# Two convolution layers on one core: another placing of rows on partitions in the first layer, and loads, stores and masks moved in the second

## The reference, cut to what matters

```python
def reference(x, L0_conv_weight, L0_conv_bias, L1_conv_conv_w, L1_conv_conv_b):   # x (8, 32, 512, 512) f32
    x = x + layer0(groupnorm16(x))     # 3x3 conv on rounded int8 values, bias, rounded and clipped to int8
    x = x + layer1(groupnorm16(x))
# layer0: x_q = clip(round(v / 0.05)), w_q = clip(round(w / 0.01)); conv 3x3, padding 1;
#         out = clip(round((acc * 0.0005 + bias) / 0.1)) * 0.1
# layer1: feat = 1x1 conv of v (32 -> 32) + bias; filt = feat pooled to 5x5 for each image and channel
#         (adaptive bins; neighbouring bins share a row where 512/5 is no integer);
#         out = depthwise 5x5 conv of feat, padding 2, each image and channel with its own filt
```

## Time and profile before

| | |
|---|---|
| median of 3 runs | 6000.67 us (5993.56 to 6012.33) |
| the profiled execution | 5992.25 us |
| its span | 5990.5 us |
| busy: PE, DVE, ACT, POOL | 4829.2, 4582.7, 3994.4, 1384.6 us |
| moved by DMA | 1347.06 MB |
| first layer; between; second | 0 to 2581 us; to 2642; to 5990 |

### The profile page before, as it was taken

How to read it: one execution, slowest core, us unless ns; L and a number is a source line. 1 busy time by engine, 2 the same in 40 slices (tenths; PEclk the granted TensorE clock), 3 DMA queues, 4 the chain that set the end, 5 groups by cost and what they waited for, 6 DMA issues and landing times.

```text
span 5990.5 us, 113135 instructions
## 1 busy us (share of the span) xinstructions
PE 4829.2 (81%) x43798; PEld 3263.0 (54%) x43798; DVE 4582.7 (76%) x5363; ACT 3994.4 (67%) x2509; POOL 1384.6 (23%) x1698
## 2 busy tenths in 40 slices
PE   0767767666667767918998989989989899899899
PEld 0111111111111111207988979979979789799798
DVE  6787878777787878747887868868868778688686
ACT  1646565655555556807877868868868778688686
POOL 0111111111111111112332323323323333233233
PEclk9888878888888888958999999989999999999999
DMA  9999999999999998949999999999999999999997
GB/s 263 278 276 301 301 287 302 281 302 273 319 261 322 271 312 242 287 96 184 180 196 179 180 193 183 181 190 182 188 192 180 197 179 180 188 189 178 188 190 125
DMA packets 1065164, 1347.06 MB, mean 225 GB/s; under 512 B 78330, under 2 KB 636666, under 8 KB 1060602
## 3 DMA queue, kind: packets, MB, share of 16 engines
q1 hardware_dynamic: 749506, 657.45, 49.3%
q0 software_dynamic: 240000, 537.11, 39.9%
q10 hardware_dynamic: 75072, 144.72, 8.3%
HBM read 800.10 MB, written 538.84 MB: 224 GB/s over the span
## 4 chain that ended last, share of the span: by engine, by line
PE 48%; SPq 4%; DMA 2%; DVE 0%; issue 0%; POOL 0%; ACT 0%; DVEq 0%; POOLq 0%; ACTq 0%
PE c_tps L1074 36%; PE c_cps L1053 4%; PE c_cps L1054 4%; PE c_cps L1055 4%; SPq L851 3%; DMA c_tt<-bias_scratch 2%; SPq L871 1%; DMA c_x<-out_dram 1%; DVE c_z L998 0%; POOL c_feat L907 0%; ACT c_z L966 0%; DVE c_xr L1031 0%; POOL c_starter L904 0%; POOL out_dram L925 0%; ACT c_feat L979 0%
## 5 line engine op out<-in xcount | busy, mean ns | idle before, releaser
L1074 PE MATMUL c_tps<-c_feat,c_tt 123*128 123x256 f16 (+1 forms) x20736 | 2385.6, 273 | 169.3 <-DMA c_tt<-bias_scratch 167.5
L1074 PEld LDWEIGHTS c_tps<-c_feat,c_tt 123*128 123x128 f16 (+1 forms) x20736 | 1998.8, 98 | 428.1 <-DMA c_tt<-bias_scratch 134.8
L925 POOL DMA_DIRECT2D out_dram<-c_xr x1152 | 1056.5, 1054 | 2266.3 <-DVE c_xr L1031 2105.9
L440 PE MATMUL b_ps<-b_xq,w0main 128*128 128x512 bf16 x3072 | 950.1, 415 | 679.5 <-ACT b_q L398 540.3
L966 ACT ACTIVATE c_z<-c_x,c_rs 128x976 f16<-128x976 f32 x576 | 1150.2, 1997 | 116.1 <-DMA c_x<-out_dram 116.1
L1031 DVE TENSOR_SCALAR c_xr<-c_tps 57x1024 f32<-57x1024 f32 (+1 forms) x576 | 701.5, 1218 | 686.1 <-PE c_tps L1074 686.1
L998 DVE SCALAR_TENSOR_TENSOR c_z<-c_x,c_rs,c_z 128x976 f16<-128x976 f32 x576 | 1105.9, 1920 | 69.6 <-ACT c_z L966 47.0
L398 ACT ACTIVATE b_q<-b_ps,q_bias 128x1024 int8<-128x1024 f32 x512 | 547.6, 1115 | 787.3 <-DVE b_x L518 728.8
L988 ACT ACTIVATE c_xr<-c_tps 57x1024 f32<-57x1024 f32 (+1 forms) x576 | 639.2, 1110 | 629.0 <-PE c_tps L1074 628.9
L440 PEld LDWEIGHTS b_ps<-b_xq,w0main 128*128 128x128 bf16 x3072 | 225.6, 101 | 1351.3 <-issue 1094.1
L453 PE MATMUL b_ps<-b_xq,w0edge 64*32 64x512 bf16 x3048 | 918.5, 411 | 0.0
(11 more groups left out here) (131 smaller groups left out, 2732.2 us busy)
## 6 DMA issues: line engine op xcount, KB each, us to landing
out_dram<-b_x POOLq DMA_DIRECT2D x512, 512.0 KB, 11.2
out_dram<-c_xr POOLq DMA_DIRECT2D x576, 384.0 KB, 7.9
c_x<-out_dram SPq DMA_DIRECT2D x224, 976.0 KB, 21.9
b_stream<-in_x_dram SPq DMA_DIRECT2D x672, 256.0 KB, 12.7
b_x<-in_x_dram ACTq DMA_DIRECT2D x276, 512.0 KB, 13.3
b_x<-in_x_dram SPq DMA_DIRECT2D x276, 512.0 KB, 12.4
c_tt<-table_scratch SPq DMA_DIRECT2D x64, 576.0 KB
out_dram<-c_xr POOLq DMA_DIRECT2D x512, 72.0 KB, 9.2
```

The costliest lines, as they stand in the source:

```text
L440: return pe.matmul(ps[:, g % 3, j, :], k.w0main[:, d, :, :].rearrange("p r o -> p (r o)"), xq[:, n % XQ_SLOTS, 2 * i + j, d:d + W], start= ...
L925: pool.dma_start(out[e::2][p, 4 * s:4 * s + 4, r0 + lo:r0 + hi, :].rearrange("c h w -> h c w"), xr_rows(m, lo, hi), accum_op=ALU.add).then ...
L1074: last = pe.matmul(tps[:, s % 2, o % 4, :], tt[0:rows, o, tp, 2 * d:2 * d + 2, :].rearrange("k w m -> k (w m)"), feat[0:rows, (e * N + i) ...
```

## The change

- **First layer.** Partition 4c+r now holds channel c's rows of image quarter r (128 rows each), so that a chunk is 8 neighbouring rows of each of the four quarters. A contiguous run is 16 KB for a whole chunk and 8 KB for half of one. A chunk is loaded by two transfers of 128 partitions (1 MB each; SP the first four rows, ACT the others), the stream by one for each half, and stored by one of 2 MB.
- All taps of a row now lie in the same partition group: 9 full 128x128 matmuls a row. At the quarters' seams the row above or below comes from a halo, `xh`: twice an image three 2 KB-a-partition transfers of 32 partitions from SP, and two ACT instructions of one row.
- Masks, group matrices and the sums' bookkeeping follow the new placing. The segments of rows, and so the number of DVE instructions in the first layer, stay as they are (edges at 25, 51, 76 and 102 of 128 both before and after). In `filters` the five bins are now gathered by quarter: 40 dependent instructions in place of 13. The weights are loaded in four transfers behind the others, after a memset.
- **Between the layers.** The first two x blocks' loads, the fillings of `feat` and `z` and the start of the store semaphores move into `statistics_of_x1`.
- **Second layer.** `z` has 3 slots, ACT works 3 steps ahead, DVE 2. SP's order where the image changes: groups 0 and 1, x block, groups 2 and 3. A step's 57 rows are stored by one transfer.

```diff
-Z_SLOTS = 4
+Z_SLOTS = 3
...
-        xv = x.rearrange("b c (n j r) w -> b n r c j w", j=JB, r=4)
+        xv = x.rearrange("b c (r n j) w -> b n (c r) j w", j=JB, r=Q)
...
-        def load_chunk(eng, xv, b, n, rows):
-            s = n % X_SLOTS
-            for r in rows:
-                eng.dma_start(xt[C * r:C * r + C, s, :, :], xv[b, n, r, :, :, :]).then_inc(x_loaded[s], 16)
+        def load_chunk(eng, xv, b, n, h):
+            s, rows = n % X_SLOTS, slice(JB // 2 * h, JB // 2 * (h + 1))
+            eng.dma_start(xt[:, s, rows, :], xv[b, n, :, rows, :]).then_inc(x_loaded[s], 16)
+
+        def load_halo(eng, xv, b, h):
+            for r in range(1, Q):
+                eng.dma_start(xh[r - h::Q, :], xv[b, :, QH * r - 1 + h, :]).then_inc(halo_loaded, 16)
...
-                            for r in range(Q):
-                                sp.dma_start(xs[C * r:C * r + C, h, :, :],
-                                             next_x[b, RESIDENT + n, r, :, JB // 2 * h:JB // 2 * (h + 1), :]).then_inc(stream_loaded[h], 16)
+                            sp.dma_start(xs[:, h, :, :],
+                                         next_x[b, RESIDENT + n, :, JB // 2 * h:JB // 2 * (h + 1), :]).then_inc(stream_loaded[h], 16)
...
-                            inner(0, True, False)
-                            for d in range(3):
-                                    pe.matmul(ps[0:C, g % 3, j, :], k.w0edge[P // 2:P, d, :],
-                                    pe.matmul(ps[P - C:P, g % 3, j, :], k.w0edge[0:P // 2, d, :],
-                            inner(1, False, False)
-                            last = inner(2, False, True)
+                            for y in (1, 0, 2):
+                                for d in range(3):
+                                    last = pe.matmul(ps[:, g % 3, j, :], k.w0main[:, y, d, :, :].rearrange("p o r -> p (o r)"),
+                                                     row(2 * i + j + y - 1)[:, d:d + W], start=(y == 1 and d == 0), stop=(y == 2 and d == 2))
...
-                    for r in range(Q):
-                        pool.dma_start(x1v[b, n, r, :, :, :], xt[C * r:C * r + C, s, :, :]).then_inc(x1_stored[s], 16)
+                    pool.dma_start(x1v[b, n, :, :, :], xt[:, s, :, :]).then_inc(x1_stored[s], 16)
...
+            for j in range(2):
+                load_block(sp, buffers, j, x1v[0], j)
...
             for i in range(NBINS):
+                for r in range(Q):
+                    for m in range(NSEG):
+                        if i not in bins_of(r, m):
+                            continue
+                        quarter = k.quarter[:, r:r + 1]
...
-                    if pointwise and j == N and s in (5, 7):
-                        sp.wait_ge(band_done, count(p, e, TILES, TILES - STEPS + s - 3) + START)
-                        load_table(p, e + 1, (s - 5) // 2)
+                    if pointwise and j == N and s in (2, 4):
+                        sp.wait_ge(band_done, count(p, e, TILES, TILES - STEPS + s) + START)
+                        load_table(p, e + 1, s // 2 - 1)
+                    if s == 6 and pointwise and (j + 2 < N or another(p, e)):
+                        load_x1(sp, p, e, j + 2)
...
-                    for lo, hi in ((0, SPLIT), (SPLIT, n)):
-                        pool.dma_start(out[e::2][p, 4 * s:4 * s + 4, r0 + lo:r0 + hi, :].rearrange("c h w -> h c w"),
-                                       xr_rows(m, lo, hi), accum_op=ALU.add).then_inc(stored[m % XR_SLOTS], 16)
+                    pool.dma_start(out[e::2][p, 4 * s:4 * s + 4, r0:r0 + n, :].rearrange("c h w -> h c w"),
+                                   xr_rows(m, 0, n), accum_op=ALU.add).then_inc(stored[m % XR_SLOTS], 16)
```

More of the change, by code:

```diff
@@ L84, with bins_of, bins_of_row @@
 NG = len(GROUPS)
+def bins_of(r, seg):
+    t = J_SEGS[seg][0]
+    assert all(bins_of_row(QH * r + t) == bins_of_row(QH * r + u) for u in range(*J_SEGS[seg]))
+    return bins_of_row(QH * r + t)
+def bins_of_row(row):
+    return [i for i in range(NBINS) if edges(i)[0] <= row < edges(i)[1]]
 SEG_GROUPS = [[g for g, t in enumerate(GROUPS) if t[3] == n] for n in range(NSEG)]
@@ L116, in _ @@
+            for r in range(Q):
+                sp.dma_start(w0f[r::Q, r, :, :], w0.rearrange("o c h w -> c o (h w)")).then_inc(spread, 16)
         @block.gpsimd
         def _(pool):
[L120 to L135, removed]
@@ new lines, in blocks @@
+            def blocks(mask, view, rows, pattern, value):
+                pool.memset(mask[:, :], value).then_inc(pool_chain, 1)
+                steps[0] += 1
+                for sign, base in ((1, 0), (-1, rows - 1)):
+                    pool.wait_ge(pool_chain, steps[0])
+                    m = view(mask[:, :])
+                    pool.affine_select(out=m, in_=m, compare_op=ALU.is_ge, fill=0.0, base=base,
+                                       pattern=[[sign * a, b] for a, b in pattern],
+                                       channel_multiplier=sign).then_inc(pool_chain, 1)
+                    steps[0] += 1
@@ L150, in link @@
                 dve.wait_ge(chain, steps[0])
-            dve.memset(k.w0main[:, :, :, :], 0.0)
-            dve.memset(k.w0edge[:, :, :], 0.0)
+            dve.memset(w0f[:, :, :, :], 0.0).then_inc(zeroed, 1)
             dve.memset(k.wh[:, :, :], 0.0)
             link(dve.memset(k.wf[:, :, :], 0.0))
-            for i in range(NBINS - 1):
-                for r in range(Q):
[L159 to L162, removed]
             for a in range(NBINS):
@@ L606, in _ @@
             gs.vector_means(dve, 0, own)
+            for slot in range(2):
+                dve.memset(feat[96:P, slot, 1, :, :], 0.0).then_inc(filled, 1)
             gs.vector_spread(dve, 0, own)
@@ L610, in _ @@
             dve.tensor_copy(rstd[:, :], gs.rstd[:, :])
-            dve.tensor_copy(mean[:, :], gs.mean[:, :]).then_inc(kept, 1)
+            dve.tensor_copy(mean[:, :], ps[:, 2, 0:nb]).then_inc(kept, 1)
+            for t in range(Z_SLOTS):
+                dve.memset(z[:, t, :, :, MAIN:P].rearrange("p b c d -> p (b c) d"), 0.0)
             dve.wait_ge(kept, 1 + START)
@@ L754, in _, with __init__, sb, rows_in @@
             sp.wait_ge(stored, 16 * (5 * lots + 1))
-def depthwise(nc, nb, k, rstd, table_d, bias_d, out):
+class BlockBuffers:
+    def __init__(self, nc, ctx):
+        def sb(name, shape, dt):
+            return ctx.enter_context(nc.sbuf_tensor(name, shape, dt))
+        self.xt = sb("c_x", [P, 2, ROWS_IN, P], F32)
+        self.z = sb("c_z", [P, Z_SLOTS, 2, PAIRS_PART, P], F16)
+        self.feat = sb("c_feat", [P, 2, 2, C, FP], F16)
+        self.starter = sb("c_starter", [P, XR_SLOTS], F32)
+        self.x1_loaded = [ctx.enter_context(nc.semaphore(f"c_x1_loaded{i}")) for i in range(2)]
+        self.stored = [ctx.enter_context(nc.semaphore(f"c_stored{i}")) for i in range(XR_SLOTS)]
+def rows_in(i):
+    return (2 if i == 0 else 0), min(ROWS_IN, H + 2 - ROWS_OUT * i)
+def load_block(eng, buffers, slot, x1, i):
+    lo, hi = rows_in(i)
+    r0 = ROWS_OUT * i - 2
+    for q in range(Q):
+        eng.dma_start(buffers.xt[C * q:C * q + C, slot, lo:hi, :], x1[q, :, r0 + lo:r0 + hi, :]).then_inc(buffers.x1_loaded[slot], 16)
+def depthwise(nc, nb, k, rstd, buffers, table_d, bias_d, out):
     with ExitStack() as ctx:
```

301 lines of the change are left out of this document (173 added, 128 removed).

## The result

The changed kernel takes 5950.0 us (median of 6 runs, 5939.1 to 5970.4) against 6001.6 (6 runs): a ratio of 0.9917, 95% interval 0.9898 to 0.9936. It is 0.8% faster, where 5.9% was forecast and 5560 us was the near end of the range, 5850 the far one. The span of the profiled execution falls by 45.7 us, from 5990.5 to 5944.8.

What follows compares the result with a forecast made beforehand. Transfers were taken to bound the streaming images, PE the last. From 5992.25 us, -20 - 279 + 56 + 2 - 38 - 74 = -353 gave 5639, and 8.4 for the runs' median gave 5647 us, range 5560 to 5850.

Steps and rivals of the forecast that it cites:

- One store of 57 partitions: Second layer: storing a step's rows in one transfer costs nothing while it ends within 21 us.
- rival 3: Second layer: the 57-partition store runs on few DMA engines, 18 to 28 us, costing beyond about 20; chance 0.10 for slower.
- PE's pitch and floor: First layer: full matmuls 0.215 us apart, so every image takes at least 247.7 + 21.4 = 269 us.
- the last image: First layer's final image, which streams nothing: grows from 213 to 269 us, a loss of 56 us.
- Transfers in the first layer: Streaming images: longer runs put transfers below PE's floor, 277 us an image for 316.8, -279 us over seven.
- The line through packet sizes: First-layer DMA: 27 ns plus 0.041 ns a byte per packet, giving 295 GB/s at 2 KB, 361 at 8 KB.
- First pass and start: First layer's beginning: first pass 100 us for 120, -20; start +2 for weights and a wider rounding.
- Between the layers: Statistics and filters: +13 fillings, +9 filters, -41 earlier first split; with block 2's x -19, sum -38 us.
- the 27 instructions: Added dependent instructions in `filters`, 0.29 us each with gaps of 0.04: +9 us.
- The second wait, for block 2's x: Second layer's beginning: ACT's 19.3 us wait for that block's load taken as gone, -19 us.
- Change of image: Second layer: SP's new order moves PE's table wait from step 2 to step 4, 7 x 10.6 = -74 us.
- the lookahead: Second layer: `z` with 3 slots and ACT and DVE working further ahead, priced at zero.

Runs made afterwards that it cites:

- kernel 8: Changed kernel with stores as 48 and 9, first-layer transfers over 128 partitions but every second row (stores every fourth), runs of 2 KB: 5632.5 us.
- kernels 7 to 9: Changed kernel, stores as 48 and 9; first-layer transfers as four of 32 neighbouring partitions, 2 KB runs over 128, four of every fourth partition: 6072.3, 5632.5, 5623.0 us.
- kernel 1: Changed kernel with only the one-piece store undone, a step's 57 rows again stored as 48 and 9: 5636.3 us.
- kernel 11: Changed kernel with stores as 48 and 9, first x blocks' loads and the fillings moved from the statistics into the filters' block: 5625.5 us.

## Why the prediction was wrong, point by point

- **The step that failed** is "One store of 57 partitions moves the same bytes; while a step's store ends within the cycle of 4 `xr` slots, 4 x 5.3 = 21 us, it costs nothing". A store costs its largest engine's share of the rows, not its bytes. 57 has no divisor between 3 and 19, so 3 of 16 DMA engines carry it; alone it takes 16.5 us, in the kernel 19.5 to landing. The condition was wrong as well: 19.5 is below the cycle of 21, and it still cost 314 us in the changed kernel and 324 in the kernel before. In the changed kernel's trace a slot's cycle has, besides the store, 1.2 us of writing, 0.8 to POOL's issue and 0.7 from landing to the next writing (medians). That leaves 18.5 of 21.2 us for the store, and a quarter of the stores take over 20.8. It was rival 3 with its mechanism, but not with its price: by its 20 us a store of 19.5 would have been free too. I gave it 0.10, although the pair 48 and 9 in the code and the factors of 57 were both before me and no row spoke against it. At 19.5 us it left a gain of 0.8%, a case for which the range had no room.
- **PE's pitch and floor**: right. 0.216 us, image 264.6 to 269 forecast; the last image pays 51 of 56.
- **Transfers in the first layer**: the size is right (273 for 277, the floor 269 set a little high), the reason wrong. The line through packet sizes gave 361 GB/s for 8 KB and 295 for 2 KB; kernel 8 moves 2 KB runs at 387, and as fast as the image needs. What decided was how a transfer's partitions are spread (kernels 7 to 9), which I had left outside the sum. That transfers fell below PE's floor all the same, and the size with it, is luck.
- **First pass and start**: -17.5 for -18.
- **Between the layers**: -8 for -19. I let SP's eight loads of x go free. SP needs 33 us to issue them, and the block didn't end before:

```profile
2311.43 33.36 SPq L869 DMA_DIRECT2D c_x<-out_dram  x8
...
2327.82 0.90 DVE L688 COPY mean<-s_ps 128x8 f32<-128x8 f32 x1
...
2345.26 0.09 DVE L746 MEMSET f_blank<- 1x32 uint32 x1 [16.54 <-PEq L642]
```

The statistics are done at 2328.7, `filters` begins at 2345.3. The rest is 6 us better than forecast in all, the 27 instructions (9 us) as forecast. The second wait, for block 2's x, fell from 19.3 us to 3.3 in kernel 1.
- **Change of image**: 74 us were credited to the order. The order as changed is worth nothing; the lookahead, which I priced at zero, is worth 38. The x block's turn in SP's queue comes when DVE has read the last of the old one, and that comes a step earlier. With the stores in two, the second layer gained 78 us in all for the 93 forecast: 38 from the lookahead, 16 from block 2's x, and the rest in shorter waits for tables (167 to 144 us with order and lookahead undone), whose cause stays open.

With the store undone the same sum would have met 5636 with 5647. That is luck: 74 us too many for the order stand against 38 too few for the lookahead, 25 too few for the streaming images and the open rest of some 24.

## What to carry to other kernels

Before merging or cutting a transfer, factor its outermost count: in these stores the largest divisor up to 16 was the number of DMA engines that carried it, and 57 partitions took three times as long as 60. When such a transfer holds one of several slots, count the whole cycle of a slot: writing, issue, landing and the next writing. Spread a transfer over all 128 partitions, or take every fourth one; run lengths from 2 KB up made no difference that counted here. In a queue that is busy, what is put ahead delays what stands behind: moving one group gained nothing and moving two gained 24 us, so test an order before you trust it, and look first at what makes the large entry due. And a block's end waits for the engine that issues transfers, too.

## What the runs showed of the hardware that I had not expected

- A store of POOL on 3 engines gives each of the 13 others as many small packets as one of the 3 has rows: 988 in a store of 57 partitions. POOL's queue went from 240000 to 667008 packets in the kernel for nearly the same bytes, so that such a count in a profile is a sign of few engines. SP's stores have none of them.
- DVE's TENSOR_SCALAR of 0.26 us took up to 5.2 us beside POOL's fillings (kernel 11).
- 32 partitions at a distance of four load at 420 GB/s, 32 neighbours at 246.
- With PE dense in the first layer its granted clock rose from 0.83 to 0.96; with a third of its work left out it fell back to 0.87, which gives back part of what is left out.
